# Adding the adjacency term of graph attention behind the turning, from a turned adjacency

## What is computed

```python
dots = einsum('bhid,bhjd->bhij', q, k) * scale          # 8 heads of 64
m2   = mask[:, None, :, None] & mask[:, None, None, :]
dots = where(m2, dots, -big)
attn = softmax(dots, axis=-1) * LA                       # LA = LG = LD = 0.33
adj  = where(m2, adjacency_mat[:, None], 0.0)
dist = where(m2, distance_mat[:, None], big)             # both matrices are adj here
attn = attn + LG * adj + LD * exp(-dist)
out  = einsum('bhij,bhjd->bhid', attn, v)                # then @ W_out + b_out, + x, layer norm
```

## Time and profile before

| what | value |
|---|---|
| three runs, median | 2696.63 us (2696.28 to 2698.97) |
| the profiled execution's own time | 2696.7 us |
| its span in the profile | 2694.8 us |
| TensorE busy | 2599.6 us, 96% of the span |
| VectorE busy | 1837.6 us, 68% |
| ScalarE busy | 894.4 us, 33% |
| GpSimd busy | 460.7 us, 17% |
| data moved | 100.87 MB |

### The profile page before, as it was taken

One profiled execution on the slowest core, in us unless ns is written; L12 is line 12 of the kernel. 1 busy time (PEld: TensorE's weight loads), 2 busy tenths in 40 slices (PEclk: granted clock), 3 DMA queues, 4 the chain that ended last, 5 costly groups with the idle time before them and its releaser, 6 DMA issues.

```text
span 2694.8 us, 74477 instructions
## 1 busy us (share of the span) xinstructions
PE 2599.6 (96%) x30296; PEld 2180.9 (81%) x30296; DVE 1837.6 (68%) x4162; ACT 894.4 (33%) x2789; POOL 460.7 (17%) x746
## 2 busy tenths in 40 slices
PE   3999999999999999999999999999999999999998
PEld 2788888887887788788888888888888888888887
DVE  3788888887888788867647656655665765565565
ACT  2222222222222222334333333432433333343233
POOL 0222222222222222210110110111011011011101
PEclk9999999999999999999999999999999999999999
DMA  5111111111111111311011101100101110110100
GB/s 162 42 39 39 39 39 39 39 39 39 39 39 39 39 39 39 114 31 35 19 32 35 31 15 35 35 19 28 36 21 29 35 31 15 35 35 19 28 21 17
DMA packets 130125, 100.87 MB, mean 37 GB/s; under 512 B 89104, under 2 KB 91152, under 8 KB 129808
## 3 DMA queue, kind: packets, MB, share of 16 engines
q1 hardware_dynamic: 129808, 96.30, 11.9%
HBM read 62.68 MB, written 33.55 MB: 36 GB/s over the span
## 4 chain that ended last, share of the span: by engine, by line
PE 83%; DVE 10%; ACT 3%; issue 2%; POOL 1%; SPq 1%; DMA 0%; DVEq 0%; POOLq 0%
PE ps L1270 22%; PE ps L597 17%; PE ps L1255 14%; PE ps L1273 11%; PE ps L600 8%; PE ps L589 3%; PE ps L1297 3%; PE ps L1335 1%; PE ps L1310 1%; PE ps L1342 1%; DVE R L460 1%; DVE sm L453 1%; DVE Tl L449 1%; DVE Tl L446 1%; ACT Th L331 1%
## 5 line engine op out<-in xcount | busy, mean ns | idle before, releaser
L1127 DVE TENSOR_TENSOR Tl<-ps,Th 128x256 fp32r<-128x256 f32 (+1 forms) x576 | 228.0, 447 | 86.5 <-ACT Th L1053 72.4
L940 POOL TENSOR_TENSOR Fp<-Fp,mhalf 128x1 f32<-128x1 f32 x128 | 77.9, 609 | 1189.9 <-DVE Fp L1134 1189.9
L597 PE MATMUL ps<-W1h,Th 128*128 128x512 f32 x512 | 206.5, 403 | 0.2 <-DVE Tl L417 0.2
L597 PE MATMUL ps<-W2h,Th 128*128 128x512 f32 x512 | 204.6, 400 | 0.1
L597 PE MATMUL ps<-W1l,Th 128*128 128x512 f32 x512 | 201.2, 393 | 0.0
L597 PE MATMUL ps<-W2l,Th 128*128 128x512 f32 x512 | 199.8, 390 | 0.0
L1058 ACT ACTIVATE R<-R 128x512 f32<-128x512 f32 x128 | 80.9, 632 | 352.0 <-DVE R L1168 352.0
L1082 ACT ACTIVATE E<-E,Fp 128x64 f32<-128x64 f32 x512 | 170.9, 340 | 32.6 <-DVE Fp L1202 31.3
L1194 DVE COPY QK<-ps 128x512 f32<-128x512 f32 x64 | 44.1, 690 | 167.5 <-PE ps L1255 167.5
L1255 PE MATMUL ps<-Th,Wh 128*128 128x256 f32 x512 | 147.7, 288 | 0.0
L243 POOL TENSOR_SCALAR sm<-sm 128x1 f32<-128x1 f32 x192 | 70.3, 366 | 441.9 <-DVE sm L455 244.7
(11 more groups left out here) (207 smaller groups left out, 6647.4 us busy)
## 6 DMA issues: line engine op xcount, KB each, us to landing
X<-in_x SPq DMA_DIRECT2D x64, 256.0 KB, 5.2
x<-R SPq DMA_DIRECT2D x64, 256.0 KB, 2.0
X<-x SPq DMA_DIRECT2D x64, 256.0 KB, 2.7
out<-E SPq DMA_DIRECT2D x64, 256.0 KB, 2.1
AB<-in_adj SPq DMA_DIRECT2D x512, 8.0 KB, 1.6
NX<-in_adj SPq DMA_DIRECT2D x128, 32.0 KB, 2.2
adjacent<-in_adj SPq DMA_DIRECT2D x16, 128.0 KB, 2.3
adjacent<-in_adj SPq DMA_DIRECT2D x32, 64.0 KB, 5.5
```

The costliest lines, as they stand in the source:

```text
L597: pe.matmul(out, Th[:, c, j * P:(j + 1) * P], R(j), start=(j == 0 and R is Rh), stop=False)
L940: return pool.tensor_tensor(col(c, RS), col(c, VE), mhalf[:, :], ALU.pow)
L1127: return dve.tensor_tensor(lo, ps, hi.bitcast(F32), ALU.subtract)
```

## The change

The adjacency term moves from the untransposed side of `ta` to the turned side. `ta` now turns `softmax * LA` alone, and the one instruction that takes all of it out of PSUM, on VectorE, adds the term. Since the term must now be turned as well, it is built from `AT`, which is turned already: `CT` has half the columns of `Cm` (one graph's 64 and not both graphs' 128, since what lies off a graph's own block is not used behind the turning). So

- `sm` on VectorE loses its last addition, `ta` on VectorE becomes a 128x512 addition out of PSUM in place of a 128x256 copy, and ScalarE's part of `ta` is gone;
- the eight loads of `A` are gone; three loads join the masks (`mrowT`, twice, and a third column set of `mcol`);
- `cm` on ScalarE casts one more small mask and takes `exp` of 256 and not 512 columns; on GpSimd one small product is added, the last three instructions get half as wide, and `BS` comes before them;
- `exp` and the product with `LG` wait for `at_ok`, and the next `at` waits for these two, since they read `AT`;
- the wait for `cm_ok` moves from `sm` to `ta`;
- SyncE's loop is written out as Python, with constants in its waits.

```diff
-        A, MM, BT = (per_graph(W) for W in (flat(first.NX), first.v_all[:, :], first.wa_all[:, :]))
-        Cm, BS = (per_graph(first.adjacent[:, k:k + 2, :, :].rearrange("p a c j -> p (a c j)")) for k in (0, 2))
+        MM, BS = (per_graph(W) for W in (first.v_all[:, :], first.adjacent[:, 2:4, :, :].rearrange("p a c j -> p (a c j)")))
+        MT, BT = (first.wa_all[:, k * CH * C:(k + 1) * CH * C].rearrange("p (c i) -> p c i", c=CH) for k in range(2))
+        CT = first.adjacent[:, 0, :, :]
...
-        MASK_LOADS = 2 * CH + 1 + 4
+        MASK_LOADS = 1 + 4 + 2 + 1
...
-                for c in range(CH):
-                    for y in range(2):
-                        sp.dma_start(A[y * C:(y + 1) * C, c, :, :], adj_t[bass.ds(tile + c, 1)].rearrange("a c g e -> (a c) g e"))\
-                            .then_inc(masks_in, 16)
...
+                for g in range(2):
+                    sp.dma_start(mrowT[g * C:(g + 1) * C, :, :], mask_halves[g, bass.ds(tile, CH), :].partition_broadcast(C))\
+                        .then_inc(masks_in, 16)
+                sp.dma_start(mcol[:, 2, :], mask_cols[:, bass.ds(tile, CH)], allow_slow_non_contiguous=True).then_inc(masks_in, 16)
...
-            with sp.Fori(0, iters - 1) as it:
-                t0 = sp.snap(it * CH)
+            for it in range(iters - 1):
+                t0 = it * CH
...
-                pool.tensor_tensor(MM[:, :, :, :], MM[:, :, :, :], mcf[:, :, :].rearrange("p g c -> p c g").unsqueeze(3).to_broadcast([P, CH, 2, C]), ALU.mult)\
+                pool.tensor_tensor(MT[:, :, :], MT[:, :, :], mcf[:, 2, :].unsqueeze(2).to_broadcast([P, CH, C]), ALU.mult)
+                pool.tensor_tensor(MM[:, :, :, :], MM[:, :, :, :], mcf[:, 0:2, :].rearrange("p g c -> p c g").unsqueeze(3).to_broadcast([P, CH, 2, C]), ALU.mult)\
                     .then_inc(mm_ok, 1)
-                pool.tensor_scalar(BT[:, :, :, :], A[:, :, :, :], LG, None, ALU.mult).then_inc(bt3, 1)
                 alone(mm_ok, n)
+                pool.tensor_scalar(BS[:, :, :, :], MM[:, :, :, :], MASKED, -MASKED, ALU.mult, ALU.add).then_inc(bs_ok, 1)
+                for p in range(2):
+                    pool.wait_ge(at_ok[p], n)
+                pool.tensor_scalar(BT[:, :, :], AT[:, :, :], LG, None, ALU.mult).then_inc(bt3, 1)
                 alone(exp_adj, n)
-                pool.tensor_scalar(BS[:, :, :, :], MM[:, :, :, :], MASKED, -MASKED, ALU.mult, ALU.add).then_inc(bs_ok, 1)
                 pool.wait_ge(bt3, n)
-                pool.tensor_tensor(Cm[:, :, :, :], Cm[:, :, :, :], BT[:, :, :, :], ALU.add).then_inc(cm2, 1)
+                pool.tensor_tensor(CT[:, :, :], CT[:, :, :], BT[:, :, :], ALU.add).then_inc(cm2, 1)
                 pool.wait_ge(cm2, n)
-                pool.tensor_tensor(Cm[:, :, :, :], Cm[:, :, :, :], MM[:, :, :, :], ALU.mult).then_inc(cm_ok, 1)
+                pool.tensor_tensor(CT[:, :, :], CT[:, :, :], MT[:, :, :], ALU.mult).then_inc(cm_ok, 1)
...
+                        act.copy(MT[:, :, :], mrowT[:, :, :])
                         act.copy(MM[:, :, :, :], mrow[:, :, :, :]).then_inc(row_ok, 1)
-                        act.activation(Cm[:, :, :, :], A[:, :, :, :], ACT.Exp, bias=ln_ld[:, :], scale=-1.0).then_inc(exp_adj, 1)
+                        for p in range(2):
+                            act.wait_ge(at_ok[p], each[ahead])
+                        act.activation(CT[:, :, :], AT[:, :, :], ACT.Exp, bias=ln_ld[:, :], scale=-1.0).then_inc(exp_adj, 1)
...
-                    if step == "ta":
-                        act.wait_ge(ta_psA, n[c])
-                        act.copy(AV(c)[:, 0:2 * P], psA[c][:, 0:2 * P]).then_inc(ta_sbA, 1)
...
+                        if each[ahead] > 1:
+                            dve.wait_ge(exp_adj, each[ahead] - 1)
+                            dve.wait_ge(bt3, each[ahead] - 1)
                         dve.transpose(AT[:, pair_c, :].rearrange("p c i -> p (c i)"), AB[:, pair_c, :].rearrange("p c i -> p (c i)"))\
                             .then_inc(at_ok[c], 1)
...
                         dve.tensor_tensor(EH(c), EH(c), col(c, RLA, HEADS).unsqueeze(2).to_broadcast([P, HEADS, C]), ALU.mult)\
-                            .then_inc(soft_ok, 1)
-                        dve.wait_ge(soft_ok, 3 * n[c])
+                            .then_inc(attn_ok, 1)
+                    if step == "ta":
+                        dve.wait_ge(ta_ps, n[c])
                         dve.wait_ge(cm_ok, each[ahead])
-                        dve.tensor_tensor(E4(c), E4(c), over_heads(Cm, c), ALU.add).then_inc(attn_ok, 1)
-                    if step == "ta":
-                        dve.wait_ge(ta_psB, n[c])
-                        dve.tensor_copy(AV(c)[:, 2 * P:4 * P], psB[c][:, 0:2 * P]).then_inc(ta_sbB, 1)
+                        dve.tensor_tensor(AV(c).rearrange("p (x m i) -> p x m i", x=2, i=C), scores(c).rearrange("p x n (y i) -> p x (n y) i", y=2),
+                                          CT[:, c, :].unsqueeze(1).unsqueeze(1).to_broadcast([P, 2, 4, C]), ALU.add).then_inc(ta_sb, 1)
...
                     if step == "ta":
                         pe.wait_ge(attn_ok, n[c])
-                        for x, ready in enumerate((ta_psA, ta_psB)):
+                        for x in range(2):
                             for n_ in range(2):
                                 mm = pe.transpose(ps[c][:, x, n_ * P:(n_ + 1) * P], E[:, c, x * 2 + n_, :], ident[:, :])
-                            mm.then_inc(ready, 1)
+                        mm.then_inc(ta_ps, 1)
                     if step == "av":
-                        alone(ta_sbA, n[c])
-                        pe.wait_ge(ta_sbB, n[c])
+                        alone(ta_sb, n[c])
```

More of the change, by code:

```diff
@@ L710, in convolutions_and_attention @@
     out_rows = out.rearrange("(t g) c d -> t (g c) d", g=P // C)
-    adj_t = adj.rearrange("(t g) c e -> t c g e", g=P // C)
+    mask_halves = mask_rows.rearrange("t (g j) -> g t j", g=P // C)
     adj_b = adj.rearrange("(t g) (a i) (b j) -> g b i t a j", g=P // C, a=2, b=2)
@@ L735, in flat @@
             return W[:, :, :].rearrange("p c k -> p (c k)")[:, 0:D]
-        A, MM, BT = (per_graph(W) for W in (flat(first.NX), first.v_all[:, :], first.wa_all[:, :]))
-        Cm, BS = (per_graph(first.adjacent[:, k:k + 2, :, :].rearrange("p a c j -> p (a c j)")) for k in (0, 2))
+        MM, BS = (per_graph(W) for W in (first.v_all[:, :], first.adjacent[:, 2:4, :, :].rearrange("p a c j -> p (a c j)")))
+        MT, BT = (first.wa_all[:, k * CH * C:(k + 1) * CH * C].rearrange("p (c i) -> p c i", c=CH) for k in range(2))
+        CT = first.adjacent[:, 0, :, :]
         mrow = sb("mrow", [P, CH, 2, C], U8)
-        mcol = sb("mcol", [P, 2, CH], U8)
-        mcf = sb("mcf", [P, 2, CH])
+        mrowT = sb("mrowT", [P, CH, C], U8)
+        mcol = sb("mcol", [P, 3, CH], U8)
+        mcf = sb("mcf", [P, 3, CH])
         XN, X, H = first.X, first.R[:, :, D:DH], first.R[:, :, 0:D]
@@ L789, in convolutions_and_attention @@
         (mc_ok, row_ok, mm_ok, bs_ok, exp_adj, bt3, cm2, cm_ok, b3_ok, bo_ok, z3, x3_ok, xp_ps, xph, xp_sb, v_ps, v_sb, s_ps, max_ok, nb_ok, ex_ok, soft_ok, attn_ok,
-         ta_psA, ta_psB, ta_sbA, ta_sbB, av_ps, avh, av_sb, wo_ps, z4, x4_ok) = map(sem, (
+         ta_ps, ta_sb, av_ps, avh, av_sb, wo_ps, z4, x4_ok) = map(sem, (
             "mc_ok row_ok mm_ok bs_ok exp_adj bt3 cm2 cm_ok b3_ok bo_ok z3 x3_ok xp_ps xph xp_sb v_ps2 v_sb2 s_ps max_ok nb_ok ex_ok soft_ok attn_ok "
-            "ta_psA ta_psB ta_sbA ta_sbB av_ps avh av_sb wo_ps z4 x4_ok").split())
+            "ta_ps ta_sb av_ps avh av_sb wo_ps z4 x4_ok").split())
         (bn3, mv3, ve3, rs3), (bn4, mv4, ve4, rs4) = first.norm1, first.norm2
@@ L901, in store @@
                 sp.dma_start(out_rows[bass.ds(t0 + c, 1)].rearrange("a r d -> (a r) d"), Z[c % 2]).then_inc(out_stored[c % 2], 16)
-            with sp.Fori(0, iters - 1) as it:
-                t0 = sp.snap(it * CH)
+            for it in range(iters - 1):
+                t0 = it * CH
                 for p in range(2):
                     for c in (2 * p, 2 * p + 1):
-                        sp.wait_ge(t_ps[0], sp.snap(t0 + (c + 1)))
-                        sp.wait_ge(b3_ok, sp.snap(t0 + (c + 1)))
+                        sp.wait_ge(t_ps[0], t0 + (c + 1))
+                        sp.wait_ge(b3_ok, t0 + (c + 1))
                         load_x(c, t0 + (CH + c))
-                    sp.wait_ge(at_ok[p], sp.snap(it + 1))
+                    sp.wait_ge(at_ok[p], it + 1)
                     load_blocks(t0 + CH, p)
-                sp.wait_ge(cm_ok, sp.snap(it + 1))
+                sp.wait_ge(cm_ok, it + 1)
                 load_masks(t0 + CH)
@@ L1061, in steps @@
                         if each[ahead] > 1:
-                            act.wait_ge(attn_ok, (each[ahead] - 1) * CH)
+                            act.wait_ge(ta_sb, (each[ahead] - 1) * CH)
                         else:
@@ L1065, in steps @@
```

(6 more changed lines are left out.)

4 lines of the change are left out of this document (2 added, 2 removed).

## The result

The change takes 2687.7 us (median of 9 runs, 2684.87 to 2688.39), the kernel before 2697.51 (9 runs, 2694.51 to 2700.15). The ratio is 0.9963, with a 95% interval of 0.9953 to 0.9973: 9.8 us less (7.3 to 12.7 by the interval), nearly twice the 5.4 us from which on this measurement tells a difference. The prediction was 2692.6 with a range down to 2688.0, so the result lies 0.3 us outside.

A forecast was written before the change was run, and what follows sets the result against it. TensorE, busy 96% of the span, was taken to bound the kernel, so only its waits count. 15 passes x 0.27 plus 0.1 in the last group made 4.1 us: 2696.7 - 4.1 = 2692.6 us, range 2688 to 2699.5.

The forecast's parts named there:

- the slower case: Rival on the new `ta` additions' row-and-broadcast access pattern making VectorE late before TensorE's waits: 2699.5 us or more, 8%.
- `wo.0`: TensorE step waiting for VectorE's `Tl` of `av.0`: starts 0.14 us later because additions replace copies at `ta.0` and `ta.1`.
- `t0.0`: TensorE step after `ta.2`: its stall of 0.43 us, for the transpose of `at.0`, goes; TensorE is 0.29 ahead.
- `av.2`: TensorE step behind `t0.0`: starts 0.18 us later, since it waits for VectorE's longer addition at `ta.2`.
- `g0.0`: TensorE step waiting for the `Tl` of `t0.0`: starts at 1426.53 against 1426.80, 0.27 us less in each pass.
- Two of the signs: Expected in the profile after: the wait before `wo.0` 0.14 us longer, and `g0.0` still waiting for `Tl`.
- The new wait of `av.2`: On TensorE between `t0.0` and `av.2`: a wait of 0.43 us for VectorE's addition, where none was before.
- both say 1425.96: At the `Tl` of `t0.0` before `g0.0`: ScalarE's copy and VectorE's own work both allow its start at 1425.96.
- The parts on `cm` and SyncE: Mask-bias work on GpSimd and ScalarE, and SyncE's fewer loads and written-out loop: each claimed to change nothing in time.
- the rest of the pass: Around `ta.3`, `ta.0` and `ta.1`: the longer addition fits in, and additions saved in `sm.0` and `sm.1` gain nothing.
- more is gained: Rival: no 0.14 loss at `wo.0` gives 2690.5 us; also a shorter wait before `g0.0` gives 2688; 17%.
- The end of the program: Last group: the addition before `ta.3` goes, `av.2` is 0.40 late, `ta.3`'s addition is longer: about 0.1 us less.

## Why the prediction was right and wrong

Its steps held to within 0.04 us. The new addition takes 679 to 693 ns over its 64 instructions, and two of them start 0.60 apart, so the slower case didn't come. The Trainium skill (Perfetto Trace Analysis, Optimizing Scalar/DVE Operations) gives an instruction of VectorE an overhead of about 125 ns on PSUM and 60 on SBUF. These rows don't show that difference: the addition out of PSUM has a median of 686 ns, that out of SBUF had 692. Counted from `ta.0`:

| step | forecast | measured |
|---|---|---|
| `wo.0` | +0.14 | +0.10 |
| `t0.0` | -0.29 | -0.31 |
| `av.2` | +0.18 | +0.15 |
| `g0.0` | -0.27 | -0.30 |

The run with `V` put back to a slow place (32 past a multiple of 256, the kernel before has 224) measures this mechanism by itself: 0.26 us in a pass, and 0.21% of the whole (0.12 to 0.30), 5.7 us (3.2 to 8.1) where 4.1 was forecast. Two of the signs were named wrongly. The wait before `wo.0` didn't grow from 0.62 but reads 0.57, since the `av` steps ahead of it on TensorE are as late. And the profile names no wait for `Tl` before `g0.0`, though it is there: `av.2` starts at 1521.26 and is issued in 0.48, so TensorE could go on at 1521.74, and `g0.0` starts at 1522.05, 0.56 after VectorE began that `Tl`, as before. The modelled end of `av.2`, 1521.95, covers it. The new wait of `av.2` is 0.46 by the same count, though its row says 0.25; the forecast says 0.43, but its own times give 0.47 (1425.74 less 1424.79 and the 0.48 of issue). Its "both say 1425.96" is 1425.94 for ScalarE's side. Neither slip changes the sum.

**What failed is a term that the sum doesn't have.** The parts on `cm` and SyncE cost the new tiles and loads at nothing, and "the rest of the pass" holds no word on products that the diff doesn't touch. `Vh` and `Vl` moved by 288 bytes, from 224 past a multiple of 256 bytes from `Th` to a multiple, and their 48 products in a pass became 3 to 5 ns faster each by their rows, 0.26 us together by the pass: 15 times, 3.9 us of the 9.8. With this term the forecast would have been 4.1 + 3.9 = 8.0 us less, 2688.7, inside its own range and inside the measured 7.3 to 12.7. The trace of before held the sign: `Vh` with `Tl` at 395 ns beside `W1l` with `Tl` at 389, a product of the same shape. I compared no rows of one shape with different names. The rival "more is gained" had the size (2688) and the wrong reason: it counted on a loss at `wo.0` that doesn't arise and on a shorter wait at `g0.0`.

What is left over is not shown to be an effect. 15 x 0.52 us is 7.8, inside the interval. In the two profiles, passes that are some tenths longer than the rest take 1.7 us before and 0.3 in the change. The end of the program gives 1.2 where 0.1 was forecast: at `ta.3` of the last group the wait of 1.29 is gone as forecast, and `av.2` and `av.3` there wait 0.88 each. But that stretch lasts 59.65 us in the change's profile, 59.04 in its repeat and 61.49 in the run with everything 64 bytes further, with the same schedule (before: 60.84), so 1.2 can't be read as the change's. In both kernels one set of 8 products with `W2l` in it is much longer than the 2.06 to 2.09 of its like, at a lower granted clock (0.62 from 2668 to 2672 us in the change, 0.70 from 2683 to 2687 before) and behind waits of 0.8 to 1.0 us, and it isn't the same set:

```profile
2684.26 3.45 PE L1270 MATMUL ps<-W2l,Th 128*128 128x512 f32 x8 [1.03 <-DVE Tl L1127]
```

in the kernel before, and in the change

```profile
2668.97 3.66 PE L1278 MATMUL ps<-W2l,Th 128*128 128x512 f32 x8 [1.03 <-DVE Tl L1133]
```

## What to carry to other kernels

When a trace shows products of one shape with different mean durations, compare where their operands lie: an unused tile of 32 bytes won here as much as the whole rearrangement. After any edit that adds or resizes a tile, compare the durations of untouched instructions first, or a gain or a loss is put down to the wrong cause; an edit of the layout and an edit of the schedule are best timed apart. And a wait that is removed can come back a few steps on: count from one fixed point to the next, and follow what the next one waits for through every engine. Here the wait for GpSimd's root took back half or more of two improvements.

## What the runs showed of the hardware

The profile shows a weight load (PEld) for every matmul; its operand is called the stationary one here, the other, whose columns are counted, the moving one. A matmul of 512 columns with `Tl` as the stationary operand takes 389 to 391 ns here when the two lie a multiple of 256 bytes apart in SBUF, and 394 to 395 at distances of 32, 64, 128 and 224 past one. With 256 columns, where three kinds of products alternate, `Tl,Wl` and `Th,Tl` take 283 at such a multiple and 280 to 282 at 64 or 128 past. Between the layouts with all distances at a multiple and the one with `W1`, `W2`, `Wh` and `Wl` 64 past, this spans 25 us, 1%. That the two reads meet somewhere would explain that the distance counts and the place doesn't, but no run shows it. The Trainium skill says (TensorE: Matmul & The Clock Gate, Step-by-step: what each phase is for) that TensorE reads the two operands through independent ports, and that loading the next weights takes no bandwidth from the running matmul. The traces can't show ports, but they do show that the time of a product depends on the distance between its two operands, by 5 ns in 390.

The granted clock differs between executions of nearly the same program. At 1.00 TensorE has its upper level, 2.4 GHz; a mean below 1 holds time at the lower one, 1.2 GHz. In the windows view from 1139 to 1149 us (busy time of PE, PEld, DVE, ACT and POOL, then the clock), behind the waits at the transition from the first half to the second, the change shows

```profile
1139.00:1149.00 10.00, 9.04 (x140) 7.61 (x144) 5.78 (x17) 2.18 (x6) 0.80 (x2) 0.83 0.46 159
```

and the kernel before

```profile
1139.00:1149.00 10.00, 9.15 (x161) 7.59 (x162) 7.09 (x20) 3.29 (x10) 1.06 (x3) 1.00 0.47 161
```

with fewer products done in the change's window. In the ten us from 1130 on TensorE was busy for 7.28 us in the one and 7.41 in the other. The repeated run of the change has 1.00 there, and reaches its first `qk.0` at 1286.55 and not 1288.95. The clock is thus likely a part of such differences of 1 to 2 us between single profiles, and so I read the effects from the passes.
